# A four-layer gated transformer: the sixteen half layer norms computed with tokens in partitions

## The reference

```
for L in 0..3:
    x = x + tanh(g_xattn[L]) * cross_L(layernorm(x), ctx)
    x = x + tanh(g_ffn[L])   * moe_L(layernorm(x))
layernorm(x) = (x - mean(x)) / sqrt(var(x) + 1e-5)      # over the 128 channels, no gain, no bias
```

## Time and profile before

| | before |
|---|---|
| three runs, median (lowest to highest) | 604.1 us (602.66 to 604.46) |
| the profiled execution's own time | 602.64 us |
| its span, first to last instruction | 600.9 us |
| mean granted clock of TensorE | 0.994 |
| TensorE matmul busy | 565.9 us, 94% |
| TensorE weight load busy (overlaps) | 392.2 us, 65% |
| VectorE busy | 447.4 us, 74% |
| ScalarE busy | 414.2 us, 69% |
| GpSimd busy | 104.0 us, 17% |
| chain of waits by engine | PE 70%, DVE 13%, ACT 12%, issue 4%, POOL 1% |

### The profile page before, as it was taken

How to read it: one execution, slowest core, us unless ns; L and a number is a source line. 1 busy time by engine, 2 the same in 40 slices (tenths; PEclk the granted TensorE clock), 3 DMA queues, 4 the chain that set the end, 5 groups by cost and what they waited for, 6 DMA issues and landing times.

```text
span 600.9 us, 8811 instructions
## 1 busy us (share of the span) xinstructions
PE 565.9 (94%) x3304; PEld 392.2 (65%) x3304; DVE 447.4 (74%) x696; ACT 414.2 (69%) x579; POOL 104.0 (17%) x69
## 2 busy tenths in 40 slices
PE   7999999989999999999897989999998998999997
PEld 5667887856777777775231337466546776788886
DVE  4367987878658899887989875766677836887786
ACT  4779899936756556657999965434514856988885
POOL 5400000011210000003989813100000310000000
PEclk9999999999999999999998999999998999999999
DMA  6208120200200812020000026306410100802000
GB/s 237 65 11 314 36 70 1 75 2 2 75 1 4 316 42 71 2 70 1 5 2 1 1 71 181 102 2 196 120 36 1 53 21 2 314 36 71 35 1 35
DMA packets 16782, 40.27 MB, mean 67 GB/s; under 512 B 1834, under 2 KB 6058, under 8 KB 16740
## 3 DMA queue, kind: packets, MB, share of 16 engines
q1 hardware_dynamic: 16740, 39.71, 19.8%
HBM read 39.01 MB, written 0.70 MB: 66 GB/s over the span
## 4 chain that ended last, share of the span: by engine, by line
PE 70%; DVE 13%; ACT 12%; issue 4%; POOL 1%; ACTq 0%; DVEq 0%; POOLq 0%
PE ps L712 38%; ACT work L1093 6%; PE ps L755 4%; DVE h_lo L1606 3%; PE ps L452 3%; PE ps L738 2%; PE ps L584 2%; PE ps L469 2%; PE ps L740 2%; PE ps L739 2%; PE ps L555 2%; PE ps L569 2%; PE ps L459 2%; PE ps L694 1%; PE ps L446 1%
## 5 line engine op out<-in xcount | busy, mean ns | idle before, releaser
L1606 DVE TENSOR_TENSOR h_lo<-h_act,h_hi 128x512 fp32r<-128x512 f32 (+1 forms) x136 | 118.3, 874 | 41.9 <-ACT h_hi L1138 41.2
L712 PE MATMUL ps<-n_hi,w_hi 128*128 128x512 f32 (+1 forms) x232 | 85.9, 404 | 4.7 <-ACT h_act L1124 1.8
L1138 ACT CAST h_hi<-h_act 128x1024 fp32r<-128x1024 f32 (+1 forms) x88 | 75.3, 856 | 13.3 <-PE ps L712 11.0
L712 PE MATMUL ps<-n_hi,w_lo 128*128 128x512 f32 (+1 forms) x232 | 83.1, 392 | 0.0
L712 PE MATMUL ps<-n_lo,w_hi 128*128 128x512 f32 (+1 forms) x232 | 83.0, 391 | 0.0
L1814 POOL TENSOR_TENSOR rstd<-var_eps,minus_half 128x4 f32<-128x4 f32 x16 | 17.8, 1113 | 317.4 <-DVE var_eps L1270 317.4
L712 PE MATMUL ps<-h_hi,w_hi 128*128 128x512 f32 (+1 forms) x184 | 65.6, 399 | 2.6 <-DVE h_lo L1606 2.6
L712 PE MATMUL ps<-h_hi,w_lo 128*128 128x512 f32 (+1 forms) x184 | 64.1, 391 | 0.0
L712 PE MATMUL ps<-h_lo,w_hi 128*128 128x512 f32 (+1 forms) x184 | 64.0, 390 | 0.0
L1093 ACT ACTIVATE work<-work,p_rest 128x2048 f32<-128x2048 f32 x31 | 59.4, 1996 | 0.4 <-DVE work L1466 0.4
L1131 ACT ACTIVATE h_act<-ps 128x512 f32<-128x512 f32 (+1 forms) x48 | 28.6, 596 | 39.1 <-PE ps L712 39.1
(11 more groups left out here) (234 smaller groups left out, 1020.4 us busy)
## 6 DMA issues: line engine op xcount, KB each, us to landing
work<-g_rows SPq DMA_DIRECT2D x36, 512.0 KB, 6.4
w_f<-in_w SPq DMA_DIRECT2D x20, 512.0 KB, 3.6
w_f<-in_w SPq DMA_DIRECT2D x8, 544.0 KB, 3.6
work<-in_w SPq DMA_DIRECT2D x2, 512.0 KB, 4.4
work<-g_rows SPq DMA_DIRECT2D x4, 256.0 KB, 9.4
p_rest<-in_p_rest SPq DMA_DIRECT2D x1, 714.0 KB, 9.9
p_attn<-in_p_attn SPq DMA_DIRECT2D x1, 546.5 KB, 6.9
x<-in_xT SPq DMA_DIRECT2D x1, 512.0 KB, 3.6
```

The lines of the kernel that those rows point to most:

```text
L712: mm = pe.matmul(dst[i], wap(wt, e, lo, size, rows), mv[i], start=(first and c == 0), stop=(last and c == 2))
L1138: act.copy(places(h_hi, m, step), places(h_act, m, step)).then_inc(s["hi"], 1)
L1606: dve.tensor_tensor(lo, src, hi.bitcast(F32), ALU.subtract).then_inc(s["lo"], 1)
```

## The change

The half-norm is computed with tokens in partitions. TensorE transposes x in four 128x128 pieces to PSUM (`norm_turn`). VectorE takes mean and variance of each token with four `bn_stats` and four `bn_aggr` and adds eps (`norm_stats`); GpSimd's power stays. VectorE subtracts the mean and multiplies by `rstd`, both a scalar per partition, in four pieces to SBUF (`norm_rows`, into `sq`). TensorE transposes back to PSUM (`norm_back`). `norm_high` and `norm_low` read that PSUM bank, and a new ScalarE copy `norm_keep` writes `n` for those that read it later (queries, features, logits, updates). `cen`, `var_w`, `norm_mean`, `norm_var`, `norm_spread`, `norm_square`, `norm_copy`, `norm_eps` and `norm_out` are gone.

```diff
+            def norm_turn(j, t):                                   # TensorE
+                if j:
+                    pe.wait_ge(x_done[t], j)
+                else:
+                    pe.wait_ge(in_x[t], 16)
+                for i in range(HT):
+                    c = t * HT + i
+                    mm = pe.transpose(ps[:, LNBANK[j, t][0], i * P:(i + 1) * P], x[:, c * P:(c + 1) * P], ident)
+                mm.then_inc(ln["turn"], 1)
+            def norm_back(j, t):
+                pe.wait_ge(ln["rows"], 2 * j + t + 1)
+                for i in range(HT):
+                    c = t * HT + i
+                    mm = pe.transpose(ps[:, LNBANK[j, t][1], i * P:(i + 1) * P], n_rows[:, c * P:(c + 1) * P], ident)
+                mm.then_inc(ln["back"], 1)
+            def norm_stats(j, t):                                  # VectorE
+                dve.wait_ge(ln["turn"], 2 * j + t + 1)
+                for i in range(HT):
+                    ins = dve.bn_stats(bn[:, t, i], ps[:, LNBANK[j, t][0], i * P:(i + 1) * P])
+                link(ins)
+                for i in range(HT):
+                    ins = dve.bn_aggr(mv[:, t * HT + i], bn[:, t, i])
+                link(ins)
+                r = slice(t * HT, (t + 1) * HT)
+                dve.tensor_scalar(var_eps[:, r], mv[:, r, 1], EPS, None, ALU.add).then_inc(ln["eps"], 1)
+            def norm_rows(j, t):
+                dve.wait_ge(ln["rstd"], 2 * j + t + 1)
+                for i in range(HT):
+                    c = t * HT + i
+                    ins = dve.tensor_scalar(n_rows[:, c * P:(c + 1) * P], ps[:, LNBANK[j, t][0], i * P:(i + 1) * P],
+                                            mv[:, c, 0:1], rstd[:, c:c + 1], ALU.subtract, ALU.mult)
+                ins.then_inc(ln["rows"], 1)
+            def norm_keep(j, t):                                   # ScalarE
+                act.wait_ge(ln["back"], 2 * j + t + 1)
+                if j % 2 and (j, t) != (5, 0):
+                    act.wait_ge(ln["lo"], 2 * (j // 2) + t + 1)
+                act.copy(n[:, half(t)], ps[:, LNBANK[j, t][1]]).then_inc(ln["n"], 1)
...
```

Where the parts are called. Attention 0, on TensorE and VectorE:

```diff
                     queries(0, 0)
-                    norm_mean(2, 1)
-                    norm_var(2, 1)
+                    norm_turn(2, 1)
                     scores(0, 0)
-                    norm_spread(2, 1)
+                    norm_back(2, 1)
                     scores(0, 1)
...
                     query_rows(0, 0)
-                    norm_eps(2, 1)
+                    norm_stats(2, 1)
                     soft(0)
-                    norm_out(2, 1)
+                    norm_rows(2, 1)
                     soft(1)
```

The start of a MoE, TensorE (the ungated branch; the gated one has up(0), logits(0), up(1), norm_back(3,1), up(2), logits(1)):

```diff
                     pe.wait_ge(ln["lo"], 2 * L + 1)
-                    up(0)
-                    up(1)
+                    for step in range(4):
+                        up(step)
+                    if L == 0:
+                        pe.wait_ge(pre["kcp"], 3)
+                    logits(m, 0)
+                    if L == 0:
+                        prepare_keys(0, 1, 1)
+                    norm_back(2 * L + 1, 1)
                     if L == 0:
                         prepare_values(0, 2)
-                    else:
-                        norm_spread(7, 1)
-                    up(2)
-                    up(3)
                     logits(m, 1)
                     pe.wait_ge(ln["lo"], 2 * L + 2)
```

```diff
-            for t in range(2):
-                norm_mean(0, t)
...
+            for t in range(2):
+                norm_turn(0, t)
+            keep_busy(6, 7)
+            norm_back(0, 0)
             pe.wait_ge(in_ctx, 16)
             pe.wait_ge(in_pack["p_attn1"], 16)
             prepare_values(0, 0)
             prepare_values(0, 1)
-            pe.wait_ge(ln["xc"], 2)
-            norm_mean(1, 0)
+            norm_turn(1, 0)
             prepare_keys(0, 0, 0)
-            norm_var(1, 0)
+            norm_back(0, 1)
             prepare_keys(0, 0, 1)
...
             prepare_keys(0, 1, 0)
+            norm_turn(1, 1)
+            norm_back(1, 0)
```

More of the change, by code:

```diff
@@ L253, in flamingo @@
         x_done = [sem("x_done0"), sem("x_done1")]
-        ln = {k: sem(f"ln_{k}") for k in ("mean", "xc", "sq", "var", "eps", "rstd", "bc", "n", "hi", "lo")}
+        ln = {k: sem(f"ln_{k}") for k in ("turn", "eps", "rstd", "rows", "back", "n", "hi", "lo")}
         pre = {k: sem(f"pre_{k}") for k in ("kv", "scan", "proj", "k", "v", "vcp", "kcp", "txt", "txtcp", "uv", "uvcp", "uv_dram", "uv_in", "wo")}
@@ L480, in norm_rest @@
             def norm_rest(j):
-                norm_spread(j, 0)
-                norm_mean(j, 1)
+                norm_turn(j, 1)
                 if j == 3:
@@ L609, in attention @@
                     scores(1, 0)
-                    norm_mean(6, 1)
+                    norm_turn(6, 1)
                     scores(1, 1)
-                    norm_var(6, 1)
                     keep_busy(2, 4)
-                    norm_spread(6, 1)
+                    norm_back(6, 1)
                 for p in range(PAIRS):
@@ L669, in pair_sums @@
                     if g == 8:
-                        norm_spread(4, 1)
+                        norm_back(4, 1)
                     if g == 9:
@@ L682, in pair_sums @@
                     if g == 25:
-                        norm_mean(5, 0)
-                    if g == 26:
-                        norm_var(5, 0)
-                    if g == 27:
-                        norm_spread(5, 0)
+                        norm_turn(5, 0)
                     if g == 28:
+                        norm_back(5, 0)
+                    if g == 29:
                         logits(MOES[2], 0)
@@ L809, in moe @@
                     up(4)
-                    norm_mean(5, 1)
+                    norm_turn(5, 1)
                     up(5)
-                    norm_var(5, 1)
                     up(6)
                     up(7)
-                    norm_spread(5, 1)
+                    norm_back(5, 1)
                     up(8)
@@ L1213, in moe @@
                         high(step - 1)
-                    if L == 0 and step in (1, 4):
-                        copy_values(0, 2 + step // 4)
+                    if step == 1:
+                        norm_keep(2 * L + 1, 1)
+                        if L == 0:
+                            split_hi_down(m, 1)
+                    if L == 0 and step in (2, 4):
+                        copy_values(0, 1 + step // 2)
                     if step == 3:
```

213 lines of the change are left out of this document (87 added, 126 removed).

## The result

The changed kernel took 625.9 us (median of 4 runs, 625.1 to 632.3) where the kernel before took 604.3: a ratio of 1.038, 95% interval 1.034 to 1.043. Beside later experiments it stood at 1.038 again (e11, 1.035 to 1.040). The direction was forecast, the size was not: +21.6 us for +3, and 625.9 lies far above the range's end of 611.0. The profiled execution took 625.1, its span is 623.3 against 600.9.

A forecast was written before the change was run, and what follows sets the result against it. TensorE was taken to bound the kernel, with 70% of the chain. Place-by-place delays summed to +3.05 us on the profiled 602.64, so 605.7; the median lies 1.5 higher: 607.2 us, range 599.8 to 611.0.

The forecast's parts named there:

- (5,1): Norm 5, second half, start of MoE 2: norm_back starts later behind VectorE's rows, logits wait 0.45 for norm_keep: +1.5 us.
- Stats: VectorE's four bn_stats, four bn_aggr, eps and links per half-norm: 1.55 us, bounds 0.8 and 2.5.
- The pair sums: Between MoE 1 and MoE 2: VectorE's rows, norm_high and norm_keep delay the first routing: +0.6 us.
- scores(0,1) after norm_back: Start of attention 0: norm_back waits for rows, these scores run after it, queries come later: +1.2 us.
- up(0) closer to the last x update: Starts of MoE 1 and 3: the first up starts some 2.5 us early, then second logits wait for norm_keep.
- MoE 3: End of attention 1 and start of MoE 3: first up 2.5 us early, second logits wait for norm_keep: +0.3 us.
- Rival B: Stats cost only 0.8 us, 0.75 less at five places where VectorE decides: 603.5 us, no change; chance 0.18.
- The head: Kernel's start through MoE 0's down loop: first up at 21.9 us, loop at 30.6: +0.7, best -2.5, worst +2.5.
- The rows: VectorE's four 128x128 scalings per half-norm, priced by a 128x128 PSUM operation of 0.29 us: 0.92 us.
- norm_back(3,0): End of attention 0: it ends where the last projection could start anyway; with MoE 1's start, -1.2 us.
- the tail of MoE 1: Last downs of MoE 1: VectorE's rows end 277.0, and the features start 0.35 us earlier.
- C: Clock rival: TensorE idles before norm_back, 1.2 GHz spells in attention 0 and head cost 1.5 us each: 610.2; chance 0.14.

The follow-up runs named there:

- e11: The changed kernel measured once more, unedited, beside the other experiments: 626.5 us, 1.038 of the kernel before.
- e1: Changed kernel with each half's four 128x128 scalings made one 128x512 instruction (result no longer the norm): 617.3 us, 1.023 of the kernel before.
- e3: Changed kernel without bn_stats and bn_aggr, constants in their place (result no longer the norm): 621.1 us, 1.029 of the kernel before.
- e4: Changed kernel with the second half's norm_keep right behind norm_high on ScalarE, the n_lo subtraction waiting for it: 619.8 us, 1.026 of the kernel before.
- e6: Changed kernel with three reorderings: scores(0,1) ahead of norm_back, project(1) ahead of norm_back, MoE 2's up(8) and up(9) ahead of norm_back: 618.0 us, 1.022.
- e10: e7 with norm_keep(4,0) behind hidden(47), 3 fills for 8 there, and 10 idle matmuls before scores(0,0): 605.8 us, 1.0045 of the kernel before.
- e12: e10 with attention-start scalings between a softmax's maximum and subtraction, earlier MoE 2 scalings and third value copy, some reordering, fewer fills: 602.9 us, 0.997.
- e13: e10 with all 52 added idle matmuls taken out, orders and copies as there: 611.6 us, 1.010 of the kernel before.
- e7: Changed kernel with e6's reorderings, norm_keep early at every MoE start as in e4, and idle matmuls in remaining waits: 611.0 us, 1.011.
- e2: Changed kernel with idle matmuls in TensorE's queue where it waits for rows or norm_keep: 616.4 us, 1.023 of the kernel before.
- e5: Kernel before, with unread VectorE work added inside each half-norm (four bn_stats, four bn_aggr, three products): 638.5 us, 1.057.

## Why the forecast was right in sign and wrong in size

**Right.** That TensorE would stand for VectorE's rows, longest in the attentions and at (5,1): 5.5, 3.9 and 2.8 us. That the work on it shrinks while the latency grows. Stats: 1.55 forecast; 0.88, 0.38 and 0.17 with links give 1.51. VectorE's time: +26 forecast, +30.3 measured. The pair sums: +0.6 and +0.5. scores(0,1) after norm_back, up(0) closer to the last x update, by 2.8 us in MoE 1 and 2.6 in MoE 3, then a wait for norm_keep: all there. Rival B's bn_stats 0.1 apart is refuted: 0.2 apart.

**The head, the largest miss:** +4.9 where the forecast had +0.7, and +2.5 at worst. The first up began at 24.0 us for the 21.9 of the forecast, the down loop at 34.2 for 30.6. Ahead of the first up, three blocks of scalings were 0.44 us longer each, and scan(0) ended at 10.3 for 9.6. The 1.5 us more on the way to the loop are the spell from 24.8, and a second one, from 35.0, follows. So the head failed by the price of the scalings (next) and by the clock.

**The rows, mis-sized.** "Four scalings, as the 128x128 row: rows = 0.92" was 1.36. The row taken (0.29) has the same shape, but a scaling with two column scalars takes 0.40 and the next follows 0.32 later. That is 7 us of VectorE, and 0.44 at each place where norm_back waits; e1 shows such time coming back one for one, e3 that it need not. At 0.44 for each of some ten such waits, my estimate is 4 to 5 of the 19 us missing.

The Trainium skill (VectorE: DVE Perf Modes, "The TRN2 errata"), weighed ahead of the run, has a formula by which 128 elements out of PSUM take 0.26 us, an estimate of that page. The trace agrees for bn_stats (0.28 with one operand out of PSUM), and not for the scaling (0.40).

**Norm_keep, mis-placed.** "The logits wait 0.45 for norm_keep" at (5,1), and +0.3 for MoE 3. norm_keep waits until norm_low has read the same bank, norm_low waits for norm_high and stands in VectorE's queue (at (5,1) behind a product), and the second logits come behind all of them. TensorE waited 1.1, 1.4 and 2.3 us there (MoE 0, 2, 3); at (5,1):

```profile
388.38 0.68 DVE L1258 TENSOR_TENSOR n_lo<-ps,n_hi 128x512 fp32r<-128x512 f32 x1
389.14 0.58 ACT L898 COPY n<-ps 128x512 f32<-128x512 f32 x1 [1.18 <-DVE n_lo L1258]
...
389.78 1.07 PE L474 MATMUL ps<-p_rest,n 128*128 128x16 f32 x8 [1.44 <-ACT n L898]
```

e4 took most of these waits away and 6 us came back.

**Norm_back ahead of project(1).** "norm_back(3,0) ends where the last projection could start anyway" failed. In attention 1 the last output's copy ended at 504.7, and project(1) began at 506.96, behind norm_back, which had waited for rows:

```profile
506.05 1.12 PE L466 MATMUL ps<-p_first,sq 128*128 128x128 f32 x4 [1.67 <-DVE sq L1250]
506.96 1.06 PE L591 MATMUL ps<-sq,p_rest 128*128 128x512 f32 x1
```

Part of the early up(0) was given back before it was had; at the end of attention 0 and the start of MoE 1 e6 shows -1.2 for +0.3, and e10, e12 and e13 -1.8 to -1.9 (e7 only +0.7, with a spell of 6.8 us in attention 0). In the tail of MoE 1 the same fault was on ScalarE: norm_keep ahead of hidden(47), 3.2 us idle. I had walked VectorE and TensorE through that place and not ScalarE.

**The clock, mis-counted.** C had the mechanism, the place (norm_back's idle time in the attentions and the head) and the side, with a chance of 0.14 and two spells at 1.5 us. The price was right (1.6 for the one read above), the count was not. There were nine where before had three (one of each at the very end), 27.7 us more at 1.2 GHz. The fills alone gave back 9 us, so some 9 of the 22 hang on it, but not all: e2's runs at a clock of 0.991 to 0.994 took 615.2 to 615.5, still 12 over. The two can't be split cleanly, since a shorter wait also saves a spell: orders and copies without any fill (e13) gave back 17.

The Trainium skill (TensorE: Matmul & The Clock Gate, "HAM oscillation — how this bites in real kernels") says that idle stretches between bursts let the clock fall and that the next burst starts at half speed. The traces agree: 1.11 us for four transposes behind a wait of 3.87 us. That transposes don't hold the clock up (the Trainium skill, the same page, "Part 4: PE-mode transpose") no run here tells apart, since the spells looked at have idle time near them.

**The sum.** The walk took each place's own delay and added them with the rest unchanged. It left out that ten waits in a row each cost the wait, and then the slow stretch behind it. What stays open: why 13.6 busy us in e3 ran at 1.2 GHz; and the head in e12.

## What to carry to other kernels

Moving work from the busiest engine into the latency between two of its steps need not be a gain, even where the other engine is a quarter idle: here 30 us more on VectorE made the kernel 3.8% slower, and 37 us more in the old order (e5) cost 35. When a step gets a longer chain, move what stands behind it on each of the three queues ahead of it first (matmuls that need nothing from it, the copies, the subtraction halves); that, with idle matmuls in the waits that stay, turned 1.038 into 0.997. Price an unseen instruction by a row of the same operand kinds, not of the same shape alone, and give every new wait of over a us or two the price of a spell at the lower clock.

## What the runs showed of the hardware that was not expected

- A scaling of 128x128 out of PSUM with two column scalars takes 0.40 us and follows the last after 0.32; one of 128x512 takes 0.81 (e1). A 128x128 product with one reciprocal operand takes 0.29.
- bn_stats of 128x128 takes 0.28 us from PSUM and from SBUF alike (changed kernel and e5), four take 0.88; bn_aggr 0.15, four take 0.38.
- TensorE stayed at 1.2 GHz through 13.6 us without idle time (e3).
- Less work can cost more: e3, with 18.9 us less on VectorE, was slower than e1, with 8.8 less (621.1 and 617.3), and spent 49 to 56 us at 1.2 GHz for 34 to 42.
- A VectorE product of 128x128 with both operands in SBUF takes 0.28 us, but six of 48 took 0.82 to 3.12 beside a GpSimd subtraction or sum, ending 0.15 after it (e5). Scalings out of PSUM beside a GpSimd sum took 0.39 to 0.40 (changed kernel).
